# Attention and a quantised feed-forward on one core: unrolled loops, a clock warm-up, the causal mask moved from TensorE to VectorE, and a feed-forward on integer weights

## The chip, the cores and the metric

One core of a Trainium2 chip runs the kernel. The metric is device time in microseconds (us) from launch to end; lower is better. Three plain runs of the kernel before are shown, and one profiled execution, whose trace is read here.

## The reference, cut to what matters

```
x: (8, 512, 128)   w_qkv: (128, 384)   w_gate, w_up: (384, 128) int32   w_down: (128, 384) int32
q, k, v = split(x @ w_qkv, 3)                     # 16 heads of 8
att = softmax(where(causal, q k^T / sqrt(8), -inf))
x = layernorm(x + att v)
gate = x @ (w_gate / 127)^T ; up = x @ (w_up / 127)^T
x = layernorm(x + (silu(gate) * up) @ (w_down / 127)^T)
```

All in float32; both layer norms have eps 1e-5 and no weights.

## The kernel before, in words

Every engine has its instruction stream written out by hand, and semaphores join the streams. Nothing is scheduled by a planner. The work has two phases.

**Attention.** The 8 batches have 16 heads each; four heads make a group, so there are 32 groups (`G`, four to a batch, `n` is the group in its batch). For each group TensorE computes scores twice. First it makes them with the queries on the partitions, only to take each row's maximum: `maxima` fills ten PSUM banks in turn (`k` = 0 to 9, in three real banks `mx_ps`), VectorE's `reduce_group` takes the maxima of each, GpSimd's `split_negmax` splits the negated maximum into two parts, TensorE turns them (`turn_negmax`), ScalarE copies them out, and a DMA (`load_negmax`) puts them as extra rows beside the queries. Two groups later (`LAG`) TensorE makes the scores again with the keys on the partitions and the maximum already subtracted (`scores`, five slots `s` of two banks), ScalarE takes the exponential of a slot (line 563, into `pt`), GpSimd zeroes what lies over the diagonal (`clear_diagonal`, line 843), and TensorE multiplies by the values (`values`, line 376). A column of ones in `vx` gives the row sums. Every second group VectorE divides by them (`normalise`), once a batch GpSimd adds the input (`add_attention`, line 850).

The ten banks of a group hold 16 blocks of 128, 256, 384 or 512 keys (`max_blocks`): banks 0 to 3 one block of 512, banks 4 to 7 one of 384 and one of 128, banks 8 and 9 two of 256. VectorE reduces a bank with one instruction, by chunks of 128 or 256 keys. So that keys behind the query don't count, `maxima` ends each bank with two small matmuls of the constant `tri` (line 366), which add -3e38 over the diagonal of each block.

TensorE's order in a group, `group(...)`, is by slot: `scores` of slot s, `maxima` of banks 2s and 2s+1 of the group two ahead, then in slot 1 `turn_negmax` and the first quarter of `values`, in slot 2 `turn_out` (every second group) and the second quarter, in slot 3 the projections of a later batch (`X`: `project_qk`, or `project_v` with `turn_x`), in slot 4 the rest of `values`. Bank 4 of the maxima uses the PSUM bank of bank 3, since `turn_negmax` and `turn_out` use the other two in between; the others wait for the bank three before.

Two groups' maxima are taken before the first scores (`group(-2)`, `group(-1)`). q and k go through HBM to be laid out as extra terms (`write_parts`, `read_rows` on SyncE's queue); their low parts are made on VectorE (`low_parts`, line 645).

**Feed-forward.** Batches `c` = 0 to 7. VectorE takes the statistics of layer norm 1 (`stats1`) and normalises (`norm1`, line 737), GpSimd takes the inverse deviation (`inverse_deviation`, lines 875 and 877). TensorE turns x1, ScalarE copies it to `x1T`, TensorE makes gate and up in plain float32 (lines 509 and 511, three chunks of 128 hidden units each), ScalarE applies silu, VectorE multiplies (line 747, `hid`), TensorE makes `down` (line 520), VectorE adds x1 and takes statistics (lines 755, 717, 721), and GpSimd normalises (`norm2`, line 885) for the store. GpSimd scales the int32 weights by 1/127 at the start (line 815).

Attention's and the feed-forward's middle batches are hardware loops (`bodies` and `whole_batches` with `Fori`), in which waits and addresses go by registers; the last batches are written out.

## Time and profile before

| | |
|---|---|
| median of 3 runs | 442.48 us (441.56 to 464.72) |
| the profiled execution's own time | 435.57 us |
| its span, first to last instruction | 433.9 us |
| TensorE busy, share of the span | 91% |
| VectorE, ScalarE, GpSimd busy | 64%, 50%, 39% |
| mean granted TensorE clock | 0.895 |

The span and the own time differ by 1.7 us, which lies around the instructions. The profiled execution is 7 us under the median. Matmuls are pipelined, so a busy TensorE isn't one at its peak. [...]

### The profile page before, as it was taken

Reading aid. Unit: us, or ns where it says so; the run is one execution under the profiler, and the core shown is the slowest. Engines: PE = TensorE matmul, PEld = TensorE weight load, DVE = VectorE, ACT = ScalarE, POOL = GpSimd, SP = SyncE. Lnnn points to the kernel's source line nnn. Section 1 sums busy time; section 2 is a strip of 40 time slices with the busy share of each in tenths; the row PEclk is TensorE's granted clock in tenths of the full one; section 3 lists DMA queues with packets and bytes.
Section 4 is the critical chain, followed back from the end, with each engine's and each line's share of the span. In section 5 each row is a group of like instructions: output and inputs, shape, how many; then the busy total and the mean of one; then the engine's idle time right before and its main releaser. Section 6 shows DMA issues by size and latency. Waiting matters only on the chain.

```text
span 433.9 us, 9906 instructions
## 1 busy us (share of the span) xinstructions
PE 393.8 (91%) x3245; PEld 231.4 (53%) x3245; DVE 277.9 (64%) x596; ACT 216.3 (50%) x277; POOL 169.1 (39%) x305
## 2 busy tenths in 40 slices
PE   5289989999999999999999999999999879999990
PEld 3157454455655555555555555555555435576560
DVE  4167434655586777767776876777777336777741
ACT  2114433545475667666566666656666653322220
POOL 8921211222323243333224334223422543776664
PEclk9655655865799999999999999999999999999997
DMA  5820560052505432540543354055100000001001
GB/s 171 264 73 5 215 200 26 4 201 93 148 4 198 132 114 105 188 147 2 196 148 97 130 163 147 2 199 168 53 4 5 26 2 2 25 25 48 26 24 48
DMA packets 33880, 41.48 MB, mean 96 GB/s; under 512 B 3136, under 2 KB 17472, under 8 KB 33856
## 3 DMA queue, kind: packets, MB, share of 16 engines
q1 hardware_dynamic: 33856, 41.17, 29.5%
q8 instruction: 14, 0.23, 0.2%
q14 instruction: 10, 0.08, 0.1%
HBM read 21.76 MB, written 18.87 MB: 94 GB/s over the span
## 4 chain that ended last, share of the span: by engine, by line
PE 70%; DVE 14%; issue 5%; DMA 4%; ACT 2%; SPq 2%; POOL 1%; DVEq 0%; POOLq 0%
PE psum L376 16%; PE psum L357 14%; DVE nm L666 11%; PE psum L346 10%; PE psum L520 5%; PE psum L509 5%; PE psum L511 5%; PE psum L322 5%; PE psum L366 4%; PE psum L312 2%; PE psum L334 2%; DMA scr_k<-parts 2%; PE psum L328 2%; DVE attn L677 1%; DMA xa<-L_attn_x 1%
## 5 line engine op out<-in xcount | busy, mean ns | idle before, releaser
L666 DVE TENSOR_REDUCE nm<-psum 128x1 f32<-128x512 f32 (+2 forms) x320 | 201.1, 684 | 98.6 <-PE psum L366 98.6
L563 ACT ACTIVATE pt<-psum 128x1024 f32<-128x1024 f32 x160 | 159.7, 1024 | 97.7 <-PE psum L346 97.0
L843 POOL TENSOR_SCALAR_AFFINE_SELECT pt<-pt 128x512 f32<-128x512 f32 x128 | 78.9, 634 | 160.0 <-ACT pt L563 159.3
L357 PE MATMUL psum<-kx,qx 33*128 33x128 f32 (+3 forms) x512 | 111.6, 379 | 18.7 <-DMA kx<-scr_k 7.7
L376 PE MATMUL psum<-pt,vx 128*32 128x512 f32 (+3 forms) x1024 | 96.3, 475 | 1.2 <-ACT pt L563 1.0
L346 PE MATMUL psum<-qx,kx 35*128 35x384 f32 (+3 forms) x512 | 88.3, 392 | 0.8 <-DVE parts L645 0.5
L357 PEld LDWEIGHTS psum<-kx,qx 33*128 33x128 f32 x512 | 67.3, 208 | 31.3 <-DVE nm L666 15.9
L346 PEld LDWEIGHTS psum<-qx,kx 35*128 35x128 f32 x512 | 47.3, 202 | 67.1 <-issue 41.8
L366 PE MATMUL psum<-tri 64*128 64x128 bf16 (+1 forms) x640 | 67.6, 227 | 0.0
L366 PEld LDWEIGHTS psum<-tri 64*128 64x128 bf16 x640 | 32.9, 105 | 24.0 <-issue 20.1
L376 PEld LDWEIGHTS psum<-pt,vx 128*32 128x32 f32 x1024 | 24.6, 112 | 21.5 <-issue 7.4
L631 ACT ACTIVATE sg<-psum 128x512 f32<-128x512 f32 x24 | 14.3, 597 | 38.2 <-PE psum L509 38.2
L850 POOL TENSOR_TENSOR res<-res,attn 128x512 f32 (+1 forms) x8 | 10.2, 1272 | 41.5 <-DVE attn L677 21.8
L885 POOL TENSOR_SCALAR yo<-r,mv,rstd 128x128 f32<-128x128 f32 x32 | 25.1, 796 | 2.1 <-POOL rstd L877 2.1
L509 PE MATMUL psum<-x1T,wT 128*128 128x512 f32 x48 | 24.7, 596 | 0.7 <-ACT x1T L623 0.7
L511 PE MATMUL psum<-x1T,wT 128*128 128x512 f32 x48 | 24.5, 592 | 0.0
L520 PE MATMUL psum<-wT,hid 128*128 128x128 f32 x192 | 22.7, 275 | 0.0
L520 PEld LDWEIGHTS psum<-wT,hid 128*128 128x128 f32 x192 | 22.1, 192 | 0.5 <-issue 0.5
L747 DVE TENSOR_TENSOR hid<-psum,sg 128x512 f32<-128x512 f32 x24 | 16.5, 686 | 9.0 <-PE psum L511 8.6
L322 PE MATMUL psum<-xT,wqkv 128*128 128x512 f32 x32 | 20.8, 786 | 0.8 <-ACT xT L542 0.8
L645 DVE TENSOR_TENSOR parts<-psum,parts 128x512 fp32r<-128x512 f32 x16 | 11.1, 691 | 11.8 <-ACT parts L549 11.4
L877 POOL TENSOR_TENSOR rstd<-veps,minus_half 128x4 f32<-128x4 f32 x16 | 16.5, 1034 | 1.3
(58 smaller groups left out, 246.3 us busy)
## 6 DMA issues: line engine op xcount, KB each, us to landing
scr_q<-parts SPq DMA_DIRECT2D x16, 512.0 KB, 3.2
scr_k<-parts SPq DMA_DIRECT2D x16, 512.0 KB, 4.6
qx<-scr_q SPq DMA_DIRECT2D x64, 128.0 KB, 2.8
kx<-scr_k SPq DMA_DIRECT2D x64, 128.0 KB, 2.8
xa<-L_attn_x SPq DMA_DIRECT2D x8, 256.0 KB, 3.0
res<-L_attn_x SPq DMA_DIRECT2D x8, 256.0 KB, 3.5
out<-yo SPq DMA_DIRECT2D x8, 256.0 KB, 2.3
qx<-nm_T SPq DMA_DIRECT2D x64, 8.0 KB
```

The lines of the kernel that those rows point to most:

```text
L322: pe.matmul(pair[:, n, :], wqkv[:, C * n:C * n + C], xT[:], start=True, stop=True).then_inc((q_made, k_made)[n], 1)
L346: last = pe.matmul(pair[:, bank % 2, col:col + width], kx[u][at:at + KS, 2 * g + hh // 2, P * j:P * j + P].bitcast(F32R), qx[u][at:at + KS ...
L357: pe.matmul(bank[:, col:col + width], qx[u][at:at + KM, 2 * g + hh // 2, P * i:P * i + P].bitcast(F32R), kx[u][at:at + KM, 2 * g + hh // 2 ...
L366: last = pe.matmul(dst, tri[at:at + 64, part, :], mask, start=False, stop=(part == 1), skip_group_check=True)
L376: last = pe.matmul(pv_ps[VW * hh:VW * hh + VW, P * j:T], vx[u][:, at:at + VW], pt[g % 2][:, bank, col:col + T - P * j], start=(j == 0 and ...
L509: pe.matmul(psum[:, 1 + k % 2, :], wT[:, 0, P * m:P * m + P], x1T[u][:], start=True, stop=True).then_inc(gate_full, 1)
L511: pe.matmul(psum[:, 3 + k % 2, :], wT[:, 1, P * m:P * m + P], x1T[u][:], start=True, stop=True).then_inc(up_full, 1)
L520: last = pe.matmul(psum[:, 5, C * n:C * n + C], hid[:, m, P * n:P * n + P], wT[:, 2, P * m:P * m + P], start=(m == 0 and n == 0), stop=(m ...
L563: act.activation(pt[g % 2][:, 2 * s:2 * s + 2, :], next_pair(), ACT.Exp, scale=SM_SCALE).then_inc(exp_done, 1)
L666: dve.tensor_reduce(dst, src, AX.X, ALU.max, negate=True).then_inc(mx_reduced, 1)
L843: pool.affine_select(out=blocks, in_=blocks, pattern=[[0, HG], [1, P]], compare_op=ALU.is_ge, fill=0.0, base=0, channel_multiplier=-1).the ...
L885: pool.tensor_scalar(yo[u][:, n, :], r2[:, n, :], mv[:, 1, n, 0:1], rstd[:, 1, n:n + 1], ALU.subtract, ALU.mult).then_inc(yo_made, 1)
```

## The change

**No loops.** `bodies` and `whole_batches` are plain Python loops: every wait is against a constant. Otherwise the attention streams keep their order.

**Inputs sooner.** The loads of x for batches 2 and 3 are issued behind batch 0's `read_rows`, and that of batch b + 4 in group 1 of batch b. Before, batch b + 2 was loaded in group 0 of batch b.

**Zero products first.** `keep_busy(n)` issues n matmuls of zeros (bf16, 128 x 128 by 128 x 512) into the bank of the values: 8 ahead of the first maxima, 3 in each slot of groups -2 and -1, 1 in each slot of group 0. The turning of the feed-forward weights moves ahead of the first maxima; their conversion and the clearing of `vx` move from GpSimd to VectorE.

**The mask.** `tri` and its matmuls are gone. VectorE takes each of the 16 blocks by an instruction of its own that reads PSUM and a mask, adds them, writes the sum times -1 to `masked` (bf16, four buffers) and takes the minimum into `nm`.

**Feed-forward.** The weights stay whole numbers (no 1/127; silu gets it as a scale, and `residual2` as 1/127 squared). x1 is split in two parts, `x1_hi` (ScalarE) and `x1_lo` (VectorE), and gate and up are each two matmuls of type float32r in place of one of float32. `down` of batch c - 1 goes behind the first chunk of batch c, with `hid` in two buffers and x1 in three. `norm1` moves from VectorE to GpSimd; both norms add a negated mean (`minus_mean`, one more small instruction) where they subtracted the mean.

```diff
-                diag = [(col + P * i) // P for _, i, col in blocks]
-                diagonal = bank.rearrange("p (m c) -> p m c", c=P)[:, diag[0]:NB:max(1, diag[-1] - diag[0]), :]
-                for part in range(2):
-                    dst = diagonal[:, :, 64 * part:64 * part + 64]
-                    mask = tri[at:at + 64, 2 + part, 0:64 * len(diag)].rearrange("p (m c) -> p m c", c=64)
-                    last = pe.matmul(dst, tri[at:at + 64, part, :], mask, start=False, stop=(part == 1),
-                                     skip_group_check=True)
                 last.then_inc(mx_full, 1)
...
+            def keep_busy(n):
+                for _ in range(n):
+                    pe.matmul(pv_ps, zeros[:, 0:P], zeros[:], start=True, stop=True, skip_group_check=True)
...
-                dve.tensor_reduce(best[:, :, 5], best[:, :, 0:3], AX.X, ALU.min).then_inc(nm_made, 1)
+                    blocks = max_blocks(k)
+                    for n, (hh, i, col) in enumerate(blocks):
+                        width = P * (i + 1)
+                        count = HG * NB * M + blocks_to(k) + n
+                        if count > 3:
+                            dve.wait_ge(mx_reduced, count - 3)
+                        dve.tensor_tensor_reduce(masked[count % 4][:, 0:width], bank[:, col:col + width],
+                                                 mask[:, T - width:T], -1.0, 3.0e38, ALU.add, ALU.min,
+                                                 best[:, hh, 3 + i:4 + i]).then_inc(mx_reduced, 1)
...
+            def ffn(c, u, first, last_one):
+                gate_up(c, u, 0, first)
+                if not first:
+                    down(c - 1, 1 - u, c == 1)
+                gate_up(c, u, 1, first)
+                if not last_one:
+                    turn_x1(c + 1, 1 - u)
+                gate_up(c, u, 2, first)
...
+            def norm1(c):
+                inverse_deviation(c, 0, mv1_made, ve1_made, mean1_made, rstd1_made)
...
+                for n in range(NB):
+                    pool.tensor_scalar(x1[c % 3][:, n, :], res[:, NB * c + n, :],
+                                       minus_mean[:, 0, n:n + 1], rstd[:, 0, n:n + 1], ALU.add, ALU.mult).then_inc(x1_made, 1)
```

**Where it moves instructions.** On VectorE, one group's maxima. Before (with the low parts of batch 0 ahead of them):

```order
L645 TENSOR_TENSOR parts<-psum,parts 128x512 x2
L666 TENSOR_REDUCE nm<-psum 128x1 x4
L666 TENSOR_REDUCE nm<-psum 128x4 x4
L666 TENSOR_REDUCE nm<-psum 128x2 x2
L668 TENSOR_REDUCE nm<-nm 128x4
```

After, from bank 3 to bank 4 of a group:

```order
L689 ISA masked,nm<-psum,mask 128x512
L689 ISA nm 128x1
L689 ISA masked,nm<-psum,mask 128x384
L689 ISA nm 128x1
L689 ISA masked,nm<-psum,mask 128x128
L689 ISA nm 128x1
```

Eleven instructions of a group become 32: each of the 16 blocks has one that goes over the block, and one that reads the result out to `nm`.

On TensorE, slot 2 of a group with `turn_out`. Before:

```order
L357 MATMUL psum<-kx,qx 128x384
L357 MATMUL psum<-kx,qx 128x128
L366 MATMUL psum<-tri 128x2x64 x2
L357 MATMUL psum<-kx,qx 128x384
L357 MATMUL psum<-kx,qx 128x128
L366 MATMUL psum<-tri 128x2x64 x2
L415 REGISTER_ALU
L312 MATMUL psum<-identf,oT 128x128 x4
L372 REGISTER_ALU
L376 MATMUL psum<-pt,vx 32x384 x4
```

After:

```order
L365 MATMUL psum<-kx,qx 128x384
L365 MATMUL psum<-kx,qx 128x128
L365 MATMUL psum<-kx,qx 128x384
L365 MATMUL psum<-kx,qx 128x128
L320 MATMUL psum<-identf,oT 128x128 x4
L377 MATMUL psum<-pt,vx 32x384 x4
```

The mask matmuls and the register instructions are gone, and nothing else has moved; a whole group loses 20 mask matmuls.

On GpSimd, one batch of the feed-forward. Before:

```order
L875 TENSOR_SCALAR veps<-mv 128x4
L877 TENSOR_TENSOR rstd<-veps,minus_half 128x4
L875 TENSOR_SCALAR veps<-mv 128x4
L877 TENSOR_TENSOR rstd<-veps,minus_half 128x4
L885 TENSOR_SCALAR yo<-r,mv,rstd 128x128 x4
```

After:

```order
L876 TENSOR_SCALAR veps<-mv 128x4
L877 TENSOR_SCALAR minus_mean<-mv 128x4
L879 TENSOR_TENSOR rstd<-veps,minus_half 128x4
L890 TENSOR_SCALAR x_1<-res,minus_mean,rstd 128x128 x4
L876 TENSOR_SCALAR veps<-mv 128x4
L877 TENSOR_SCALAR minus_mean<-mv 128x4
L879 TENSOR_TENSOR rstd<-veps,minus_half 128x4
L901 TENSOR_SCALAR yo<-r,minus_mean,rstd 128x128 x4
```

GpSimd now makes both norms of a batch, and the means' negatives.

## Rows read from the trace of the kernel before

**Rows 1.** The page: busy shares, and TensorE's granted clock in 40 slices.
```profile
PE 393.8 (91%) x3245; PEld 231.4 (53%) x3245; DVE 277.9 (64%) x596; ACT 216.3 (50%) x277; POOL 169.1 (39%) x305
...
PEclk9655655865799999999999999999999999999997
```

**Rows 2.** Windows: PE, PEld, DVE, ACT, POOL busy (instructions), clock, DMA.
```profile
70.00:80.00 10.00, 10.00 (x51) 4.68 (x44) 3.27 (x5) 3.18 (x4) 1.22 (x2) 0.52 0.01 2
...
120.00:130.00 10.00, 9.88 (x94) 5.56 (x97) 7.91 (x15) 6.99 (x11) 2.92 (x6) 1.00 0.01 4
```

**Rows 3.** Windows again: attention at full clock, and the feed-forward.
```profile
120.00:340.00 220.00, 210.43 (x2140) 121.92 (x2143) 164.67 (x294) 139.67 (x174) 74.96 (x146) 1.00 0.34 110
357.00:423.00 66.00, 65.31 (x311) 41.65 (x311) 44.79 (x172) 20.39 (x33) 40.24 (x57) 1.00 0.09 25
```

**Rows 4.** The chain of waits: `project_qk` (start us, us), once a batch.
```profile
75.72 3.73 PE psum L322 x4
...
123.74 1.93 PE psum L322 x4
...
161.43 1.93 PE psum L322 x4
```

**Rows 5.** The timeline, first and last maxima, and attention's last instructions.
```profile
20.48 2.48 DVE L666 TENSOR_REDUCE nm<-psum 128x1 f32<-128x512 f32 x4 [9.58 <-PE psum L366]
...
340.68 0.16 DVE L668 TENSOR_REDUCE nm<-nm 128x4 f32<-128x12 f32 x1
...
355.26 0.60 ACT L575 ACTIVATE oT<-psum 128x512 f32<-128x512 f32 x1 [2.48 <-PE psum L376]
```

**Rows 6.** The timeline, slots 1 and 2 of one group at full clock.
```profile
231.38 2.48 DVE L666 TENSOR_REDUCE nm<-psum 128x1 f32<-128x512 f32 x4 [0.28 <-PE psum L366]
...
233.98 0.50 PE L346 MATMUL psum<-qx,kx 35*128 35x384 f32 x4
...
234.33 0.51 PE L357 MATMUL psum<-kx,qx 33*128 33x384 f32 x4
...
234.62 0.35 PE L366 MATMUL psum<-tri 64*128 64x128 bf16 x4
...
234.89 0.85 PE L376 MATMUL psum<-pt,vx 128*32 128x384 f32 x8
234.94 1.29 DVE L666 TENSOR_REDUCE nm<-psum 128x4 f32<-128x512 f32 x2 [1.07 <-PE psum L366]
```

**Rows 7.** Groups of instructions, shapes apart (busy, mean ns, idle before).
```profile
L677 DVE TENSOR_TENSOR attn<-psum,rsum 128x256 f32<-128x256 f32 x17 | 7.2, 425 | 1.1
...
L673 DVE RECIPROCAL rsum<-psum 128x32 f32<-128x32 f32 x17 | 5.9, 346 | 8.8 <-PE psum L312 8.8
...
L805 POOL TENSOR_SCALAR tri<-tri_f 128x128 bf16<-128x128 f32 x4 | 1.1, 300 | 0.1
```

**Rows 8.** The timeline, one batch of the feed-forward.
```profile
366.16 1.02 PE L509 MATMUL psum<-x1T,wT 128*128 128x512 f32 x2
...
371.31 0.60 PE L312 MATMUL psum<-identf,x 128*128 128x128 f32 x4
...
371.75 2.84 PE L520 MATMUL psum<-wT,hid 128*128 128x128 f32 x24
...
374.43 1.02 PE L509 MATMUL psum<-x1T,wT 128*128 128x512 f32 x2
```

**Rows 9.** The timeline, the end.
```profile
423.96 0.69 DVE L755 TENSOR_TENSOR r<-psum,x 128x512 f32<-128x512 f32 x1 [1.92 <-PE psum L520]
...
425.71 0.38 DVE L721 BATCH_NORM_AGGREGATE mv<-stats 128x2 f32<-128x6 f32 x4 [0.15 <-DVE stats L717]
426.29 0.19 POOL L875 TENSOR_SCALAR veps<-mv 128x4 f32<-128x4 f32 x1 [3.16 <-DVE mv L721]
426.56 1.03 POOL L877 TENSOR_TENSOR rstd<-veps,minus_half 128x4 f32<-128x4 f32 x1
427.83 3.12 POOL L885 TENSOR_SCALAR yo<-r,mv,rstd 128x128 f32<-128x128 f32 x4 [0.24 <-POOL rstd L877]
```

More of the change, by code:

```diff
@@ L71, in max_blocks, with blocks_to @@
     return [(k - 2 * HG, 1, 0), (k - 2 * HG + 2, 1, 256)]
+def blocks_to(k):
+    return sum(len(max_blocks(n)) for n in range(k)) if k >= 0 else blocks_to(MX + k) - HG * NB
 MX_PLACE = (0, 1, 2, 3, 6, 7, 8, 9, 10, 11)
@@ L93, in attention_ffn @@
         identf = sb("identf", [P, P], F32)
-        tri_f = sb("tri_f", [P, 4, P], F32)
-        tri = sb("tri", [P, 4, P], BF16)
+        mask = sb("mask", [P, T], F32)
+        masked = [sb(f"masked{n}", [P, T], BF16) for n in range(4)]
         wqkv = sb("wqkv", [P, 3 * C], F32)
@@ L129, in attention_ffn @@
         x_in = [sem(f"x_in{u}") for u in range(2)]
-        res_in = sem("res_in")
+        res_in = [sem(f"res_in{u}") for u in range(2)]
         w_in = sem("w_in")
@@ L402, in group @@
                         for k in (2 * s, 2 * s + 1):
[L403 removed]
+                            if m > 0 or k > 2:
                                 if k == 5 and NM is not None:
@@ L538, in copy_xt @@
                 act.wait_ge(xt_made, b + 1)
-                if not (isinstance(b, int) and b == 0):
+                if b > 0:
                     act.wait_ge(k_made, b)
@@ L546, in first_parts @@
                     act.wait_ge((q_made, k_made)[n], b + 1)
-                    if n == 0 and not (isinstance(b, int) and b == 0):
+                    if n == 0 and b > 0:
                         act.wait_ge(scr_written, SCR * b)
@@ L552, in copy_v @@
                 act.wait_ge(v_made, b + 1)
-                if not (isinstance(b, int) and b < 2):
+                if b > 1:
                     act.wait_ge(pv_done, NG * b - NG)
@@ L560, in exp_slot @@
                 act.wait_ge(st_full, SLOTS * G + s + 1)
-                if s == 0 and not (isinstance(G, int) and G < 2):
+                if s == 0 and G > 1:
                     act.wait_ge(pv_done, G - 1)
@@ L567, in copy_negmax @@
                 act.wait_ge(nm_turned, m + 1)
-                if not (isinstance(m, int) and m < 2):
+                if m > 1:
                     act.wait_ge(nm_loaded, NM_LOADED * (m - 1))
@@ L654, in reduce_group @@
                         after_k7()
-                    if k == 0 and not (isinstance(M, int) and M < 2):
+                    if k == 0 and M > 1:
                         dve.wait_ge(nm_split, M - 1)
@@ L711, in body @@
                         turn[0] += 1
-            bodies(dve, body)
+            for b in range(B):
+                body(b // 2, b % 2, b + 2 < B, b + 1 < B)
             def norm_stats(src, k, st_made, mv_made, count):
@@ L803, in _ @@
-            pool.wait_ge(tri_step, n)
-            for part in range(4):
-                pool.tensor_scalar(tri[:, part, :], tri_f[:, part, :], 1.0, 0.0, ALU.mult, ALU.add).then_inc(tri_made, 1)
+            pool.affine_select(out=mask[:, T - P:T], in_=mask[:, T - P:T], pattern=[[-1, P]], compare_op=ALU.is_ge,
+                               fill=MASKED, base=0, channel_multiplier=1).then_inc(tri_made, 1)
             pool.memset(minus_half[:], -0.5).then_inc(small_set, 1)
             pool.memset(nm_parts[:], 0.0).then_inc(small_set, 1)
-            for u in range(2):
-                pool.memset(vx[u][:], 0.0).then_inc(v_zeroed, 1)
-                pool.wait_ge(v_zeroed, u + 1)
-                pool.memset(vx[u][:, 0:NB * H * VW].rearrange("p (s w) -> p s w", w=VW)[:, :, VW // 2 + D:VW // 2 + D + 1],
-                            1.0).then_inc(v_ones, 1)
@@ L813, in _ @@
-            pool.wait_ge(wff_in, 48)
-            for n in range(3):
-                pool.tensor_scalar(wdeq[:, n, :], wraw[:, n, :], W_SCALE, 0.0, ALU.mult, ALU.add).then_inc(wff_deq, 1)
-            pool.wait_ge(wff_deq, 3)
             pool.memset(qx[1][:], 0.0).then_inc(rows_set, 1)
@@ L896, in _ @@
+            def ffn(c, u, first, last_one):
+                if not (first or last_one):
+                    norm1(c + 1)
+                if not first:
+                    norm2(c - 1, 1 - u)
+            norm1(0)
+            norm1(1)
             add_attention(B - 1)
-            whole_batches(pool, ffn)
+            whole_batches(ffn)
+            norm2(B - 1, (B - 1) % 2)
 _INS = ["L0_attn_x", "L0_attn_w_qkv", "L0_ffn_w_gate", "L0_ffn_w_up", "L0_ffn_w_down"]
```

299 lines of the change are left out of this document (144 added, 155 removed).

## The prediction

> **What bounds the kernel now.** I read the page first. TensorE is busy 91% of the span, and its granted clock is half or a mixture for the first third; from about 120 us it is full [rows 1]. So two questions come before any other: what sets the pace at full clock, and what the half clock costs.
>
> At full clock [rows 3] TensorE is busy 210.43 of 220 us, VectorE 164.67. The chain of waits shows `project_qk` once a batch; two such starts in the full-clock stretch lie 161.43 - 123.74 = 37.69 us apart [rows 4], so a group takes 9.42 us. Of these TensorE is busy 9.42 x 0.957 = 9.0 and VectorE 9.42 x 0.7485 = 7.05. TensorE is the bound, but VectorE isn't far: it has 2.4 us a group left.
>
> Maxima run from 20.48 to 340.84 us [rows 5], that is 320.4 us for 32 groups; 32 at 9.42 would be 301.4. **The half clock costs 19 us.** A half-clock batch lasts 123.74 - 75.72 = 48.0 us [rows 4], though some of it already ran at full.
>
> The feed-forward repeats every 374.43 - 366.16 = 8.27 us [rows 8], with TensorE busy 65.31 of 66 us [rows 3]. From the last attention copy (355.26 + 0.60 = 355.86, [rows 5]) to the end of the span are 78.0 us.
>
> **TensorE's saving in a group.** Four mask matmuls hold the stream from 234.62 to 234.89, 0.27 us [rows 6]. A group has 12 as wide, 0.81 us, and 8 half as wide, about 0.27 us: 1.1 us. TensorE's need falls from 9.0 to 7.9 us. [...]
>
> **VectorE's cost in a group.** The order shows 16 instructions over the blocks and 16 small reads, for 11 before. The elements are the same, 4 x (512 + 384 + 256 + 128) = 5120. An addition of 512 elements from PSUM takes 0.69 us [rows 9], one of 256 takes 0.425 [rows 7]: 1.035 ns an element, 5.30 us. The fixed part depends on overlap. Two reductions take 1.29 us and four 2.48 [rows 6]: behind another one each adds 0.595, though alone one takes 1.29 - 0.595 = 0.695. So a block costs 0.595 - 0.530 = 0.065 us beyond its elements when it runs behind another, and 0.165 alone. The read isn't in the trace. The nearest rows are small instructions: 0.16 us alone [rows 5], and (0.38 - 0.16) / 3 = 0.073 us in a row of four [rows 9]. I take 0.073, since reads stand in a dense queue; the other end is 0.16, plus 0.10 more if the next block can't overlap the read either. Sum: 5.30 + 16 x (0.065 + 0.073) = 7.5 us. The low parts (2 x 0.69 a batch) and `normalise` (2 x (0.346 + 0.425), [rows 7]) add 2.92 / 4 = 0.73. VectorE needs 8.2 us, more than TensorE's 7.9: **the bound changes engine.** Behind a block that waits for VectorE stand `turn_negmax`, `values` and the next `scores` on TensorE, and behind those ScalarE.
>
> [...]
>
> **Waits that stay.** Bank 4 uses the PSUM bank of bank 3, so TensorE can't fill it until VectorE is done: from its matmul's start to VectorE's are 234.94 - 234.33 = 0.61 us [rows 6], 0.5 without the mask. Now this hides in a wait of 1.07 us; afterwards it is what is left of it. The same refill comes in every second group behind `normalise` (0.25 a group), and the value projection holds TensorE for longer than two full banks last VectorE, about 0.15 a group. A group then takes 8.2 + 0.5 + 0.25 + 0.15 = 9.1 to 9.2 us; I take 9.15, against 9.42. Most of what TensorE saves is thus spent on VectorE. Bounds from this step alone: 8.6 if the waits nearly vanish, 9.42 if they stay as they are.
>
> **The start.** First maxima wait for the round trip of q and k through HBM, which is unchanged: 20.5 us. The feed-forward weights' conversion and the clearing of `vx` go to VectorE, whose wait of 9.58 us before the first maxima [rows 5] covers them. The x loads go ahead in the queue behind `read_rows`; the first negated maximum isn't ready until later. [...] The slices fall from 0.9 to 0.5 from about 10 to 30 us [rows 1], where TensorE, like VectorE, stood still for the round trip, and after `project_qk` of 75.72 us [rows 4] they come back for a while; so I take a TensorE that is kept fed there to hold the full clock throughout, which is worth the 19 us.
>
> **Attention's sum.** 20.5, two groups of maxima alone at 7.5 + 0.5 = 8.0, thirty at 9.15 = 274.5: 311.0 us for the end of the maxima, where it was 340.84. The last two groups have no maxima on VectorE and don't change: 355.86 - 340.84 = 15.0. Attention ends at 326.0.
>
> **Feed-forward.** A float32 product of 512 columns takes (371.31 - 366.16) / 6 = 0.86 us [rows 8]. Two of float32r take its place. The nearest row is 1024 such columns of maxima in 234.62 - 234.33 = 0.29 us [rows 6], two at a time on few rows, so 512 take 0.15 to 0.29; I take 0.22. Twelve are 2.6 us (3.5 at the upper end), turning 0.44, `down` 371.75 to 374.43 = 2.68: TensorE needs 5.7 to 6.6 for 8.27. TensorE is no longer the bound. What is late next is the loop through layer norm 1: statistics until GpSimd starts, 426.29 - 424.65 = 1.6 us (424.65 is the residual's end); inverse deviation 427.83 - 426.29 = 1.54 and the new negated mean 0.2 [rows 9]; four norms; turn 0.6, copy 0.6, low part 0.69, product 0.69, and 0.6 of hand-overs. The norms are the unknown: with subtraction and per-partition operands one takes 3.12 / 4 = 0.78 us [rows 9], while a multiply and add with immediates on the same 128 elements takes 1.1 / 4 = 0.275 [rows 7]. The new form is an add and a multiply, so I take the second, 1.1 us for four. Sum 7.6; overlap at the ends makes me take 7.4. Eight batches save 8 x 0.87 = 7 us. The end saves 2.0 on four norms and pays 0.2 for the mean; the first norm, now on GpSimd behind its last mask, adds 0.5. From 355.86 on: 78.0 - 7 - 1.8 + 0.5 = 69.7 us. Span 326.0 + 69.7 = 395.7; with the 1.7 outside it 397.4. **Forecast: 398 us**, against 435.6 for the profiled execution and 442.5 for the median. The measurement can tell about 2% from no change.
>
> **Rivals.** (1) **GpSimd's norms stay slow**, since per-partition operands and not subtraction make them slow. For it: only the form with immediates is seen fast. Then GpSimd has 2 x (3.12 + 1.74) = 9.7 us a batch and is the bound at 9.8; 8 x 2.4 + 2 + 2 = 23 us more: 421 us.
>
> (2) **The read can't overlap its block** (the slower side). Place: between each of 512 pairs on VectorE, now the bound. Price: 0.16 in place of 0.073 is 0.09 us, 46 us in all, 444 us; if the next block waits as well, 0.19 us, 97 us, 495 us. In the middle, at 0.13, it is 465. It turns the change slower from 44.5 / 512 = 0.087 us a block on. For it: the result exists only after the last element. Against it: all neighbours in this trace overlap.
>
> (3) **The clock falls in mid-attention.** TensorE's busy share drops from 96% to some 86%, and the mask matmuls, which kept it fed, are gone. From 75.72 to 123.74 about 20 us were at full clock, so 28 us at half did the work of 17.7, 1.58 times as long. TensorE's 7.9 would be 12.5 us, 3.3 over a group; over half of the groups that is 50 us: 448 us. Against it: windows at half clock had TensorE busy too (10.00 of 10, [rows 2]), so its share isn't what decides, and it held from 120 us on.
>
> (4) **The mask as second operand halves the rate.** [...] It would be 5.3 x 32 = 170 us more, 567 us. [...]
>
> (5) **The waits vanish**: groups of 8.6 us and batches of 6.6: 375 us.
>
> **Chances.** Forecast 0.46 (its own range 384 to 415), rival 1 0.12, rival 2 0.20, rival 3 0.12, rival 4 0.04, rival 5 0.06. Faster by over 2% (under 433.6): the forecast, 5, nearly all of 1, half of 3 and a little of 2: 0.71. Within 2%: 0.10. Slower, over 451.3: 0.19, mostly 2 and 4. The range goes from 378, between rival 5 and the forecast, to 450, past rivals 1 and 3 and the low end of 2.
>
> **What would show it.** Clock 1.00 in nearly all slices; first maxima at 20 to 21 us; block and read together about 0.138 us over the elements; VectorE near 90% in attention with TensorE waiting for it; a batch of attention 36.6 us; four norms on GpSimd in 1.1 us; a feed-forward batch of 7.4. I am wrong if the read takes 0.16 us or holds its neighbours, or if the clock isn't full behind the first groups.

## The result, and the profile after

The changed kernel takes 491.5 us (median of four; 482.0 to 501.3), the kernel before beside it 442.0 (436.2 to 464.7). Ratios are taken between the faster executions of both kernels, here 482.0 and 485.3 against 436.2 to 442.5: 1.099, 95% interval 1.077 to 1.121. The forecast was 398 us. The kernel before scatters by itself: of its 41 executions in this study 19 took 431 to 445 us and 22 took 454 to 497, and the longer ones had the lower mean clock (444 us with 0.87, 497 us with 0.73).

The profiled execution took 482.0 us, with a span of 480.3. Its page, to be laid beside [rows 1]:

```profile
PE 435.2 (91%) x2646; PEld 237.9 (50%) x2648; DVE 298.0 (62%) x1252; ACT 217.2 (45%) x277; POOL 163.9 (34%) x325
...
PEclk9897569558999955965556555985675559899998
```

TensorE has 600 matmuls fewer in its records and was busy 41 us longer. The last row says why. Before, the clock was mixed until 120 us and then full (1.00) to the end. Now it goes up and down until 400 us. The mean is 0.74 for 0.895. Even the start, where the change has its zero products, isn't at full clock throughout (columns as in [rows 2], the clock is the third from the right):

```profile
20.00:30.00 10.00, 9.66 (x35) 3.42 (x34) 7.40 (x33) 0.00 (x0) 0.16 (x1) 0.69 0.63 171
30.00:40.00 10.00, 9.03 (x47) 4.37 (x47) 8.78 (x41) 3.32 (x5) 1.34 (x5) 0.99 0.02 4
40.00:50.00 10.00, 9.70 (x36) 4.54 (x39) 7.22 (x31) 5.43 (x7) 2.45 (x6) 0.67 0.46 171
```

In windows of 2 us it is 0.50 from 20 to 26 us, full from 28 to 38, and 0.50 again from 40 to 46. Ahead of the first maxima (19.71 us) TensorE had stood 2.83 us for the DMA of k: the eight zero products didn't reach that far.

The timeline has `project_qk` once a batch of attention, as [rows 4]:

```profile
117.82 1.98 PE L330 MATMUL psum<-xT,wqkv 128*128 128x512 f32 x4
...
154.36 1.98 PE L330 MATMUL psum<-xT,wqkv 128*128 128x512 f32 x4
...
200.58 1.98 PE L330 MATMUL psum<-xT,wqkv 128*128 128x512 f32 x4
```

The first two are 36.54 us apart, and between them the clock was full. Before, it was 37.69. The next are 46.2 us apart; later (the chain of waits, 253.49 to 305.00) it is 51.5, mostly at half clock. Windows of that one good batch and of two stretches behind it (columns as in [rows 2]):

```profile
117.82:154.36 36.54, 33.41 (x288) 17.49 (x284) 30.15 (x136) 24.05 (x31) 12.79 (x25) 1.00 0.41 132
...
166.00:194.00 28.00, 27.81 (x148) 15.12 (x148) 15.13 (x72) 11.82 (x15) 7.66 (x15) 0.51 0.37 116
...
210.00:255.00 45.00, 44.90 (x233) 23.75 (x233) 24.84 (x116) 19.04 (x23) 10.69 (x21) 0.50 0.31 98
```

Read across: at full clock TensorE is busy 91% of the time (before 96%, [rows 3]) and VectorE 83%. At half clock TensorE is busy 99 to 100% and the others wait for it: from 210 to 255 us ScalarE waits 21.8 us for the scores and VectorE 17.9 us for the maxima. So the 99 to 100% stand here with a clock of 0.50 to 0.51, and are no sign that nothing is wrong.

What TensorE did before the clock fell at about 166.1 us, in windows of 1 us:

```profile
164.00:165.00 1.00, 0.45 (x6) 0.25 (x4) 0.59 (x2) 0.76 (x1) 0.00 (x0) 1.00 1.02 377
165.00:166.00 1.00, 0.77 (x10) 0.57 (x8) 0.71 (x5) 0.68 (x2) 0.57 (x1) 1.00 1.02 379
166.00:167.00 1.00, 0.88 (x6) 0.66 (x10) 1.00 (x7) 0.61 (x1) 0.88 (x3) 0.54 1.03 383
```

This is a group without projections, in slots 3 and 4. TensorE first stood 0.55 us for `normalise` and then 0.35 us for a maximum:

```profile
164.75 0.50 PE L365 MATMUL psum<-kx,qx 33*128 33x384 f32 x4 [0.55 <-DVE attn L700]
...
166.12 0.79 PE L365 MATMUL psum<-kx,qx 33*128 33x256 f32 x2 [0.35 <-DVE nm L689]
```

In windows of 1 us the clock falls from full nine times in attention. The first three falls (39.8, 50.0, 63.7 us) are in groups with projections; the other six (84.2, 166.1, 207.0, 261.7, 319.7, 353.8 us) are all in groups without.

VectorE, the answer to [rows 5 and 6]. Each block has its pass and its small read:

```profile
20.63 0.69 DVE L689 CUSTOM_DVE_ANT_0 masked<-psum,mask 128x512 bf16<-128x512 f32 x1 [4.34 <-PE psum L365]
21.25 0.08 DVE L689 DVE_READ_ACCUMULATOR2_ANT nm<- 128x1 f32 x1
21.25 0.69 DVE L689 CUSTOM_DVE_ANT_0 masked<-psum,mask 128x512 bf16<-128x512 f32 x1
...
132.28 0.68 DVE L689 CUSTOM_DVE_ANT_0 masked<-psum,mask 128x512 bf16<-128x512 f32 x1
132.89 0.08 DVE L689 DVE_READ_ACCUMULATOR2_ANT nm<- 128x1 f32 x1
132.89 0.69 DVE L689 CUSTOM_DVE_ANT_0 masked<-psum,mask 128x512 bf16<-128x512 f32 x1
```

The pass of a full block takes 0.69 us, and the next one starts 0.61 us behind it, at the very moment at which the read starts. The passes over 512, 384, 256 and 128 elements take 687, 555, 419 and 285 ns on the mean, 134 ns for 128 elements, which is 0.54 us for 512 (the prediction's estimate was 0.53); the read takes 83 ns. With the 0.53, pass and read together cost 0.61 - 0.53 = 0.08 us over the elements.

The feed-forward, the answer to [rows 8], and its norms, the answer to [rows 9]:

```profile
429.50 0.66 PE L320 MATMUL psum<-identf,x 128*128 128x128 f32 x4 [1.29 <-POOL x L890]
...
429.91 0.48 PE L521 MATMUL psum<-x_hi,wT 128*128 128x512 f32 x1
...
437.08 0.66 PE L320 MATMUL psum<-identf,x 128*128 128x128 f32 x4 [0.94 <-POOL x L890]
...
437.49 0.48 PE L521 MATMUL psum<-x_hi,wT 128*128 128x512 f32 x1
...
475.90 1.74 POOL L901 TENSOR_SCALAR yo<-r,minus_mean,rstd 128x128 f32<-128x128 f32 x4 [0.24 <-POOL rstd L879]
```

A batch takes 437.08 - 429.50 = 7.58 us for 8.27, and TensorE now waits about 1 us in it for GpSimd's norms. Four norms take 1.74 us. Attention ends at 405.93 + 0.60 = 406.5 us (before 355.9), the whole at 480.3. The loss is all in attention.

### The profile page after: what moved, and what is told of

Same layout as the page of the kernel before. It is cut to its first block, busy times and chain, and to the rows that moved or that the text cites. A ratio compares the mean times of both kernels' runs of the same rounds, so it can differ in the third digit from the quotient of the medians.

```text
span 480.3 us, 8390 instructions
## 1 busy us (share of the span) xinstructions
PE 435.2 (91%) x2646; PEld 237.9 (50%) x2648; DVE 298.0 (62%) x1252; ACT 217.2 (45%) x277; POOL 163.9 (34%) x325
## 4 chain that ended last, share of the span: by engine, by line
PE 41%; DVE 7%; POOL 5%; issue 4%; ACT 1%; POOLq 0%; DVEq 0%
PE psum L377 14%; PE psum L354 9%; PE psum L365 9%; PE psum L320 3%; POOL x L890 3%; DVE masked L689 2%; POOL rstd L879 2%; PE psum L330 2%; DVE stats L754 2%; PE psum L342 1%; PE psum L336 1%; PE psum L533 1%; DVE pt L789 1%; ACT x_hi L647 1%; DVE mv L758 1%
## 5 line engine op out<-in xcount | busy, mean ns | idle before, releaser
L689 DVE CUSTOM_DVE_ANT_0 masked<-psum,mask 128x384 bf16<-128x384 f32 (+3 forms) x512 | 218.6, 487 | 124.9 <-PE psum L365 105.6
L365 PE MATMUL psum<-kx,qx 33*128 33x384 f32 (+3 forms) x512 | 122.2, 430 | 12.5 <-DVE nm L689 5.7
L377 PE MATMUL psum<-pt,vx 128*32 128x512 f32 (+3 forms) x1024 | 126.2, 603 | 1.0 <-ACT pt L586 1.0
L689 DVE DVE_READ_ACCUMULATOR2_ANT nm<- 128x1 f32 x512 | 42.3, 83 | 0.0
L533 PE MATMUL psum<-wT,pt 128*128 128x128 f32 x192 | 22.9, 276 | 1.5 <-DVE pt L789 1.5
L533 PEld LDWEIGHTS psum<-wT,pt 128*128 128x128 f32 x192 | 22.5, 192 | 2.8 <-DVE pt L789 2.3
L524 PE MATMUL psum<-x_lo,wT 128*128 128x512 f32 x48 | 20.4, 426 | 2.0 <-DVE x_lo L770 2.0
L521 PE MATMUL psum<-x_hi,wT 128*128 128x512 f32 x48 | 21.3, 445 | 0.7 <-ACT x_hi L647 0.7
L789 DVE TENSOR_TENSOR pt<-psum,sg 128x512 f32<-128x512 f32 x24 | 16.0, 672 | 2.9 <-ACT sg L655 2.0
L320 PE MATMUL psum<-identf,oT 128*128 128x128 f32 x68 | 15.7, 373 | 0.8 <-ACT oT L598 0.8
```

What stands on the lines that cost most here:

```text
L320: last = pe.transpose(dst[:, P * n:P * n + P], src[:, P * n:P * n + P], identf[:])
L365: last = pe.matmul(bank[:, col:col + width], qx[u][at:at + KM, 2 * g + hh // 2, P * i:P * i + P].bitcast(F32R), kx[u][at:at + KM, 2 * g + ...
L377: last = pe.matmul(pv_ps[VW * hh:VW * hh + VW, P * j:T], vx[u][:, at:at + VW], pt[g % 2][:, bank, col:col + T - P * j], start=(j == 0 and ...
L521: pe.matmul(psum[:, bank + k % 2, :], w, x1_hi[u][:].bitcast(F32R), start=True, stop=False)
L524: pe.matmul(psum[:, bank + k % 2, :], w, x1_lo[u][:].bitcast(F32R), start=False, stop=True).then_inc(full, 1)
L533: last = pe.matmul(psum[:, 5, C * n:C * n + C], hid[u][:, m, P * n:P * n + P], wT[:, 2, P * m:P * m + P], start=(m == 0 and n == 0), stop= ...
```

## The experiments

Before each expectation stands the edit. "A wide zero product" is a matmul of zeros, 128 x 128 by 128 x 512 in bf16, into the bank that `scores` is about to fill; it computes nothing that is used.

**1. Is it the clock, and which part of the change loses it?** Four kernels ran side by side.

The changed kernel with a wide zero product ahead of the scores of every slot:

```diff
             def scores(u, g, s):
                 pair = next_pair()
+                pe.matmul(pair[:, 0, :], zeros[:, 0:P], zeros[:], start=True, stop=True, skip_group_check=True)
```

> The changed kernel with one zero product more (bf16, 128 x 128 by 128 x 512) ahead of the scores in every slot of attention, in the bank that the scores then overwrite. Theory A (the clock fell since the mask matmuls no longer fill TensorE in between): the product puts as much work back, the granted clock is above 0.95 and the time is near 390 us, from groups of 7.9 to 8.5 us. Theory B (the clock falls where TensorE waits for VectorE, and filling elsewhere doesn't help): the clock stays near 0.74 and the time is 490 us or more, since the product takes 0.4 us a slot at half clock. Theory C (the unrolled streams or the new order of transfers): as B.

The changed kernel with zero matmuls in the shape and place of the mask matmuls (64 rows, in the banks of the maxima):

```diff
+                for part in range(2):
+                    none = zeros[at:at + 64, 0:64 * len(diag)].rearrange("p (m c) -> p m c", c=64)
+                    last = pe.matmul(dst, zeros[at:at + 64, 0:P], none, start=False, stop=(part == 1), ...)
```

> The changed kernel with the two mask matmuls of each bank put back in their place and shape, but with zeros in them, so that TensorE's stream is that of the kernel before while VectorE keeps the new masking. Theory A: the clock is back above 0.9 behind the start and the time is 390 to 400 us (groups of 9.0). Theory B: VectorE still makes TensorE wait, the clock stays below 0.8, and the time is 480 to 500 us. Theory C: as B.

The kernel before, its mask matmuls left out and nothing in their place, so that keys behind the query count in the maxima:

```diff
-                    last = pe.matmul(dst, tri[at:at + 64, part, :], mask, start=False, stop=(part == 1), ...)
```

> The kernel before with its mask matmuls left out, so that keys behind the query count in the maxima; all else, VectorE's reductions and the loops too, is as before. Theory A: the clock that was full from 120 us on now falls in attention, the mean is 0.70 to 0.80, and the time is 450 to 480 us although TensorE has 1.1 us a group less to do. Theory B: VectorE is as fast as it was, the clock stays full in the steady part, and the time is about 405 to 430 us. Theory C: as B, 405 to 430.

The changed kernel with VectorE's reductions of before. The maxima take no mask at all:

```diff
-                        dve.tensor_tensor_reduce(masked[count % 4][:, 0:width], ...)
+                    dve.tensor_reduce(dst, src, AX.X, ALU.max, negate=True)
```

> The changed kernel with VectorE's ten reductions a group as before and no mask at all, so that keys behind the query count in the maxima. Theory A: no change of the clock, 0.70 to 0.78, and 470 to 495 us. Theory B: TensorE waits less for VectorE, the clock is above 0.9, and the time is near 380 us. Theory C: as A.

| | median us (runs) | mean clock of each run |
|---|---|---|
| wide zero products | 427.3 (423.5 to 433.8) | 0.95 to 0.99 |
| mask-shaped zeros | 463.3 (436.4 to 478.1) | 0.80 to 0.91 |
| before, no mask matmuls | 472.3 (460.2 to 478.5) | 0.74 to 0.78 |
| after, old reductions | 471.7 (467.8 to 492.9) | 0.69 to 0.77 |
| the kernel before, same chip | 444.7 (443.0 to 497.1) | 0.73 to 0.87 |

The first kernel does more work than the changed one and is 64 us faster by the medians (all its executions are under 434 us, all of the changed kernel's over 482). Against the kernel before it is 0.956 (0.950 to 0.963). Its page and a window of its attention:

```profile
PEclk9858999999999999999999999999999998999997
```

```profile
80.00:340.00 260.00, 254.43 (x1989) 122.41 (x1988) 194.97 (x872) 161.97 (x194) 85.36 (x167) 1.00 0.32 103
```

So the clock is the loss: held at 1.00, even a kernel with more work is faster than before. The third kernel changes nothing but the mask matmuls, and in the stretch in which the clock was 1.00 before [rows 3] it is 0.73:

```profile
120.00:340.00 220.00, 211.69 (x1415) 112.10 (x1416) 139.11 (x248) 120.39 (x148) 63.59 (x124) 0.73 0.33 108
```

TensorE had less to do and a batch took 44.4 us (the chain of waits, 162.72 to 207.17) for 37.69. That all of its four executions are at a clock of 0.74 to 0.78, while about half of those of the kernel before are at 0.87 and more, makes me blame the mask matmuls' absence; one execution would not have, since the kernel before also had executions at 0.73 to 0.75. The fourth says that VectorE's new instructions aren't what loses the clock: with the old reductions it is at 0.69 to 0.77. Its median is 20 us under the changed kernel's, but the executions overlap, so a smaller share of VectorE isn't excluded. The second says that putting matmuls of that shape back isn't enough to be safe: 436 us once, 478 at worst.

**2. How much has to be put in?** In `scores`, for the changed kernel: the wide product only `if s in (0, 2, 3)`; five of 256 columns; mask-shaped zeros with 128 rows for 64. And the kernel before with 16 zero products at the start, three a slot in groups -2 and -1 and one a slot in group 0.

> The changed kernel with the wide zero product ahead of the scores in slots 0, 2 and 3 alone, three a group where the first such run had five, which held the clock at 1.00 in attention with groups of 9.95 us. Theory A (the clock needs a certain amount of work on TensorE, wherever it comes from): three are 1536 columns at 128 rows; if that is enough, the clock is above 0.95, groups take 9.1 us, and the time is 400 to 405 us; if it isn't, the clock is at 0.75 to 0.9 and the time 430 to 480. Theory A2 (what counts is that no slot runs thin): the bare slots 1 and 4 have the values, so the clock holds too, same numbers. Theory B (waits for VectorE decide, and five products only bridged them): the clock falls, 450 us or more.

> The changed kernel with a zero product of 256 columns ahead of the scores in all five slots: 1280 columns at 128 rows a group, half of the first such run. Theory A: a dose question; if half is enough, the clock is above 0.95 and groups of 8.9 us give near 395 us; if not, 0.8 and 440 to 470 us. Theory B: the clock falls, 450 us or more.

> As the run with zeros in the mask matmuls' place and shape, but the products have 128 rows in place of 64; columns, number and place are the same, so TensorE's time is too. That run sat between the states (436 to 478 us). Theory A by rows (what counts is how much of the array a product fills): the clock now holds above 0.95 and the time is 395 to 410 us. Theory A by time alone (what counts is how long TensorE streams): no difference, 435 to 478 us.

> The kernel before with the zero products of the start alone: 16 ahead of the first maxima, 3 in each slot of groups -2 and -1, 1 in each of group 0. All else is the kernel before. My forecast's term says that these 19 us come back: clock near 1.00 from 25 us on, 415 to 425 us. The rival reading, after the changed kernel fell back to half clock at 46 us though it had the same products: they lift the clock only while they last, it falls again by 50 us, and the time is 435 to 450 us, as before.

They took 485.0, 454.7, 654.4 and 476.8 us (medians), at mean clocks in the profiled executions of 0.83, 0.82, 0.64 and 0.84. None holds the clock. The 128-row form is slow even at full clock. In the timeline one bank of maxima, two matmuls in series, takes 0.32 and 0.44 us, and its zeros 0.22. In the changed kernel, with nothing between them, two banks of this shape take 0.34 us together (120.07 to 120.41 us):

```profile
309.07 0.40 PE L365 MATMUL psum<-kx,qx 33*128 33x256 f32 x2
309.39 0.29 PE L374 MATMUL psum<-zeros 128*128 128x128 bf16 x2
309.61 0.50 PE L365 MATMUL psum<-kx,qx 33*128 33x256 f32 x2
310.05 0.29 PE L374 MATMUL psum<-zeros 128*128 128x128 bf16 x2
```

From 309.07 to 310.26 us two banks with their zeros take 1.19 us. The same in the kernel with zeros of 64 rows takes 0.56 (153.41 to 153.97 us). The expectation took TensorE's time as the same for 64 and for 128 rows; it isn't. The kernel puts every second bank's operands on partitions 64 and up. In the changed kernel two products of 512 columns, one from each half, start together at 131.14 us and are done in 0.40, and one alone takes 0.49 (131.65 us). With the zeros of 128 rows the second bank's products start only at 309.61 us, 0.54 behind the first bank's: here the two banks no longer run at the same time. How much of the 654 us is this and how much the clock wasn't separated.

The last one speaks on the step that failed in my prediction. The kernel before, started with zero products, has the full clock from 30 to 42 us and loses it there again (0.57 to 0.63 from 42 to 60). Its 476.8 us (462.4 to 479.8) are no gain on the 464.7 (443.7 to 490.8) of the kernel before beside it, and neither expectation had it that slow. It also lost the clock at about 247 us, in a stretch in which TensorE did little (windows):

```profile
230.00:240.00 10.00, 9.39 (x105) 5.15 (x100) 7.50 (x14) 6.00 (x7) 2.92 (x6) 1.00 0.58 214
240.00:250.00 10.00, 4.69 (x51) 3.24 (x48) 4.05 (x8) 3.69 (x5) 2.23 (x5) 0.86 0.37 111
250.00:260.00 10.00, 10.00 (x59) 5.38 (x58) 4.50 (x8) 3.33 (x4) 2.02 (x3) 0.50 0.46 133
```

Here TensorE stood 3.4 and 1.8 us, and from 150 to 160 us, where the clock was already at 0.50, 2.37 and 1.77 us. At none of the four did it wait for a semaphore that the trace shows; the timeline calls it "issue". This kernel and the kernel before have loops. The profiled execution of the kernel before has no such stop; nor have those of the changed kernel and of two unrolled ones with wide zero products, in every slot and in both groups without projections. That the stops come from the loop's instructions, and that they make the scatter of the kernel before, fits this but was not tested.

**3. Which products, which slots, which start?** The wide products in slots 0 to 3; in both groups of a batch that have no projections (`g in (3, 0)`); in every slot but without the change's 8 + 30 + 5 zero products at the start; and in the kernel before.

> Four wide zero products a group in place of five (none in slot 4, where TensorE already has the values of two key blocks). Theory P (the clock needs the stream of TensorE without thin places, and slot 4 isn't one): the clock stays at 1.00 as with five products, and a group costs 0.3 us less where TensorE is the bound (9.95 to about 9.6): 427 - 32 x 0.3 = 418 us. Theory Q (there is no spare: a fifth product less lets the clock fall now and then, as three did): mean clock 0.85 to 0.95 and 440 to 465 us.

> Five wide zero products, but only in the groups in which no projections run (two of each batch's four), in which the clock was seen to fall. Theory P (the fall starts in those groups' thin places alone): clock 1.00 all through, two of four groups 7.9 to 8.5 us, two 9.95, attention some 20 to 25 us shorter than with products in all: about 405 us. Theory Q (groups with projections are no better fed in the mean of a stretch): the clock falls in them, mean 0.75 to 0.88, and the time is 445 to 475 us.

> The version with five wide zero products in every group, without the 8 + 30 + 5 zero products of the change at the start. Theory P (the start's products matter as such): the first groups run at half clock for 20 to 40 us more, 8 to 15 us in all: 435 to 442 us. Theory Q (what holds or raises the clock is the steady stream alone, and the start's products bring at most a few us): 427 to 431 us.

> The kernel before, with the same five wide zero products a group. Theory P (such products hold the clock in either kernel, and the kernel before loses it only where it isn't kept fed): clock 1.00 from the first groups on, a group of 9.42 + 5 x 0.3 = 10.9 us since TensorE is its bound, attention 20.5 + 32 x 10.9 + 15 = 385 us, and with 78 us behind it 465 us, with hardly any scatter between runs. Theory Q (its stops, in which TensorE waits for its own instructions, cost it the clock whatever it computes): stretches at half clock stay, and it is 480 us or more.

| | median us (runs) | clock, profiled |
|---|---|---|
| slots 0 to 3 | 455.8 (450.6 to 468.1) | 0.85 |
| groups without projections | 427.7 (415.8 to 437.0) | 0.89 |
| every slot, no products at the start | 427.5 (426.4 to 433.0) | 0.95 |
| the kernel before, every slot | 472.4 (465.4 to 475.2) | 0.90 |

Four products aren't four fifths of five: theory Q. Without the start's products the time is the same (427.5 for 427.3, though on another chip), and the profiled executions agree: `project_qk` of the same batch starts at 66.29 us without them and at 66.43 with them, although the clock is 0.50 from 20 to 40 us without. So those 43 products, the change's own means, bring nothing that can be seen here. In the kernel before the wide products cost more than they bring (472.4 us, against 457.2 for the kernel before beside it): TensorE, busy 210.43 of 220 us without them [rows 3], is its bound, and stretches at half clock stay.

The second row is the telling one. It has half as many products as the kernel of experiment 1, and its page:

```profile
PEclk9899667999999999999999999955596576999998
```

From 80 to 280 us the clock is full without a break. It falls at about 281.3 us, and it comes back late:

```profile
278.00:280.00 2.00, 2.00 (x24) 1.13 (x23) 1.93 (x13) 1.62 (x3) 1.66 (x4) 1.00 0.73 231
280.00:282.00 2.00, 1.61 (x7) 0.52 (x10) 2.00 (x7) 1.66 (x3) 0.27 (x2) 0.82 0.01 2
282.00:284.00 2.00, 2.00 (x14) 0.82 (x8) 0.23 (x2) 0.00 (x0) 0.00 (x0) 0.50 0.06 16
```

By the timeline this is slot 1 of a group of the last batch but one that has no zero products and whose value projection comes only in slot 3 (288.20 us), behind a wait of 0.27 us for VectorE. The group behind it is the first that has neither zero products nor projections, since no later batch is left to project, and the last batch (from about 318 us) has two more. The first kernel of the next pair puts products into these three, and leaves the place where the fall began as it is.

**4. The place.** Wide products in all groups without projections, the last batch's too, and in the first three groups (`if X is None or G < 3`). The same number of products, but only in the groups with projections (`g in (1, 2)`). And the changed kernel with mask-shaped zeros and the old reductions together.

> Five wide zero products in every group without projections, the last batch's groups 1 and 2 among them, and in the first two groups with projections. Theory P (the clock falls where a group has neither projections nor zero products): full clock from the first groups to the end of attention, groups of 9.95 and 7.9 to 8.5 us by turns, attention's end near 326 us, and 400 to 410 us in all, with under 2% between runs. Theory Q (what held from 80 to 280 us in the run before this one was luck of a marginal stream): stretches at half clock somewhere in 60 to 300 us, and 415 to 440 us.

> Five wide zero products only in the two groups of each batch that have projections, as many as in the run that left the clock full for 200 us, in the other places. Theory P (the groups without projections are where it falls): mean clock 0.70 to 0.78, the time 480 to 500 us, no better than the changed kernel. Theory Q (it is the number of products over a batch that counts, wherever they stand): mean clock 0.88 or more and 415 to 440 us.

> The changed kernel with both things put back that it took from the kernel before in the maxima: VectorE's reductions of whole banks, and on TensorE matmuls of zeros in the place, shape and number of the mask matmuls. It leaves out the mask's numbers in the maxima. No loops, early inputs, the start's zero products and the new feed-forward stay. Theory A (the clock is lost with the mask products): the clock is near 1.00 from 60 us on, a group 9.4 us, 425 to 440 us. Theory R (something else in the changed kernel's stream, the missing register instructions or its evener pace, also costs the clock): mean clock under 0.85 and 455 us or more.

The first took 421.7 us (417.4 to 422.0), 0.953 of the kernel before (0.939 to 0.967). The second took 490.3 (479.8 to 490.8), no better than the changed kernel with no zero products in attention's steady part. Their pages:

```profile
PEclk9899977999999999999999959999999996999998
```

```profile
PEclk9799876588555975795559555985696589899998
```

This pair tells the place, for whole groups: **the clock is mostly lost in the groups without projections**. In the second kernel's trace all seven falls behind 70 us are in such groups, as the last six of the changed kernel were. Projections are float32 products of 128 rows one behind the other (four take 1.98 us at full clock); most other products of a group are of 33 and 35 rows or 32 columns. It wasn't quite as expected: the first kernel still lost the clock at 58 and 242 us, so 421.7 in place of 400 to 410. Both falls are in groups with projections. The one at 242 is at the very place of the fall at 281.3 us above: slot 1 of a group with the value projection and without zero products, behind a wait of 0.27 us. The one at 58 is in a group that has both zero products and projections. So "without projections" is where most falls are, not a condition. The batch at full clock is 37.87 us.

The third took 455.2 us (447.5 to 456.8), on the side of theory R. Its clock was full from 130 to 285 us and half from 80 to 120 and in the last batch:

```profile
PEclk9898969555599999999999999655559858899997
```

Of its four falls before 300 us two (39.0, 59.5) are in groups with projections and two (80.0, 288.2) in groups without. Its 455.2 us lie inside what the kernel before took beside it (440.4 to 487.3, median 463.4), so this run doesn't show whether the unrolled stream with both parts put back holds the clock worse than the kernel before, or as badly. Experiment 1 points at the mask matmuls' absence; this run and its second kernel say that putting their like back doesn't make the clock safe.

**5. Down to the slot?** As the first kernel of 4, with two products more in the groups with projections: in slots 0 and 1 (`if thin or s < 2`), or in slots 3 and 4 (`if thin or s > 2`), where the projections stand.

> As the run with zero products in all groups without projections, and two more in slots 0 and 1 of the groups with projections. Theory P, down to the slot (the clock falls in the stretch that has neither projections nor zero products, which in these groups is slots 0 to 2): full clock from 40 us to the end of attention, 412 to 420 us, with hardly any scatter. Theory Q (only the number over a group counts): the same as the other kernel of this pair.

> The same number of zero products, but the two more stand in slots 3 and 4 of the groups with projections, beside the projections. Theory P, down to the slot: the clock still falls now and then in the first slots of such a group, 420 to 432 us: no better than without them (421.65) and a few us worse for their own time. Theory Q: as the other one, clock 1.00 and 412 to 420 us.

418.4 us (416.5 to 421.6) and 426.2 (423.0 to 429.7). The times are those of theory P, but the trace doesn't bear out its reason. From 80 us to the end of the maxima both have a clock of 1.00 and batches of 38.5 us, although the second leaves bare the place of the falls at 242 and 281.3 us. They differ in the first 80 us. The first fell at 45 us, but was back before 60. The second stood 2.36 us for a DMA at 57 us and ran at half clock from 59 us to past 67, where its `project_qk` took 3.78 us:

```profile
57.10 0.39 PE L351 MATMUL psum<-zeros 128*128 128x512 bf16 x1 [2.36 <-DMA qx<-nm_T]
```

```profile
56.00:58.00 2.00, 0.90 (x5) 0.40 (x5) 0.00 (x0) 0.04 (x1) 0.17 (x1) 1.00 0.49 149
58.00:60.00 2.00, 2.00 (x8) 0.85 (x6) 1.71 (x5) 1.98 (x2) 0.00 (x0) 0.75 0.95 258
60.00:62.00 2.00, 2.00 (x9) 0.20 (x8) 0.82 (x4) 0.27 (x1) 0.63 (x1) 0.50 0.43 129
```

Whether the slot within a group matters stays open. The first of the two is by its median the fastest version of this study: the slowest of its four executions (421.6) is 10 us under the fastest of the seven that the kernel before ran beside it (431.4 to 486.0).

```profile
PEclk9899699999999999999999999999999996999998
```

Where does it gain on the profiled execution of the kernel before (span 433.9)? Its attention ends at 341.51 + 0.60 = 342.1 us, not 355.9, though its batch of 38.50 us is longer than the 37.69 of before: all 13.8 us come from the start, where before ran at half clock, and the mask's move has been eaten up by the products that replace it. The feed-forward and the end take 417.0 - 342.1 = 74.9 us for 78.0.

## Why the prediction was wrong

**The step that failed** stands under "The start": "so I take a TensorE that is kept fed there to hold the full clock throughout". In the sum that put the loss of the clock in attention at nothing, and the start's gain at 19 us. Measured, the clock was 0.69 from 20 to 30 us in spite of the zero products, 0.99 from 30 to 40, and it fell in the first group that had scores to make (39.8 us) and eight times after that. Attention ended 80.5 us later than forecast (406.5 for 326.0 us). The start's products didn't decide it either way: without them, but with products in attention, nothing was lost (427.5 against 427.3 us). The prediction's own sign of being wrong, a clock that isn't full behind the first groups, is the one that came. And rival 3, which had the mechanism with its cause ("the mask matmuls, which kept it fed, are gone"), got a chance of 0.12 by two bad arguments. "its share isn't what decides" took windows at half clock with TensorE fully busy as evidence that feeding it doesn't help; but the busy share there comes with products stretched by the half clock: the four of `project_qk` take 3.73 us at 75.72 us and 1.93 at 123.74 [rows 4]. And "it held from 120 us on" was an observation of the stream with mask matmuls, used for one without them.

**Rival 3's size.** It priced a half-clock group at 3.3 us over a group, and half of the groups. Measured: (51.5 - 36.54) / 4 = 3.7 us, and the attention's excess of 406.5 - 326.0 = 80.5 us is that of 21 to 22 of the 32 groups. The price was near; the share of the groups was too small. The mechanism that it names, the missing mask matmuls, is borne out by experiment 1 as a part: no run separates what the unrolled loops and the new order of transfers do to the clock.

**The group at full clock.** Forecast 9.15 us, a batch of 36.6; measured 36.54. The sum was right by two errors. VectorE costs 0.08 us a block over the elements, not 0.138, so it is busy 30.15 / 4 = 7.5 us a group and not 8.2. TensorE is busy 33.41 / 4 = 8.35 and not 7.9. The 1.1 us that the mask matmuls were to give back came out as 9.0 - 8.35 = 0.65. The bound didn't change engine, then: TensorE is still the busier, and it stands 9.14 - 8.35 = 0.8 us a group. The gain, 1.15 us a batch, is as small as forecast.

**Rival 2 is refuted.** The read of the accumulator takes 0.083 us and starts with the next pass (21.25 us), and a pass starts while the one before has 0.07 us to go (0.69 - 0.62). Neither the read nor the next pass waits for the end of the one before, as the reductions of before didn't (0.695 us long and 0.595 apart, [rows 6]). Rival 4, the mask as second operand at half the rate, is refuted as well: a block of 512 takes 0.69 us with it, and a reduction over 512 without it took 0.68 in the kernel before.

**The feed-forward.** Forecast 7.4 us a batch, measured 7.58. The norm takes 0.447 us on GpSimd, between my 0.275 and the 0.78 of rival 1. From attention's end on it is 480.3 - 406.5 = 73.8 us, forecast 69.7: 1.4 of the 4.1 are eight batches of 0.18, 0.6 the four last norms. The rest was not taken apart; at the passage from attention TensorE stood for layer norm 1 and then ran at half clock for some 3 us:

```profile
408.00:412.00 4.00, 2.24 (x9) 1.48 (x10) 2.52 (x11) 2.43 (x3) 1.95 (x6) 0.98 0.00 0
412.00:416.00 4.00, 4.00 (x14) 2.98 (x13) 2.19 (x4) 1.85 (x4) 2.41 (x4) 0.59 0.00 0
```

**The forecast's sum** therefore held wherever the clock held: 36.54 for 36.6 a batch, first maxima at 20.6 for 20.5. It would have given 398 us plus the feed-forward's 4. What it lacked was the condition under which it was true, and no run in this study kept the changed kernel at that clock without paying 1.3 to 3.3 us a batch for it.

## What to carry to other kernels

When an edit takes work from TensorE, ask what clock the rest will run at: look at where the stream is thinnest, not at its mean, and price the half clock over most of the phase rather than as a remote case (here it was the excess of 21 to 22 groups of 32). A busy share of 99% at a clock of 0.50 was no proof here that TensorE was fed before the clock fell; compare the times of the same instructions at either clock. To test for it, put useless wide products into the stream: five a group brought this kernel from 491.5 to 427.3 us and its clock from 0.74 to 0.97, so the clock was what it had lost by. Then find the few places that need them.

## What the runs showed of the hardware

- The granted clock fell although TensorE was busy 91% in the batch before (117.82 to 154.36 us, at 1.00). The fall came in a group without projections, after waits of 0.55 and 0.35 us. The other five falls behind 70 us were in groups without projections too, the three before 70 us in groups with them.
- Five wide zero products in each of two groups of four kept the clock full for 200 us; the same number in the other two groups left it at 0.76 on the mean. One costs 0.32 us of stream (200.24 to 200.56 in the kernel of experiment 1), but a group with five took only (39.8 - 36.54) / 4 = 0.8 us more, and TensorE's idle time in a batch went from 36.54 - 33.41 = 3.1 us to 0.8 (39.00 of 39.82 us busy): a part of their time fell into waits.
- Zero matmuls of 128 rows between products of 33 rows: two banks of maxima with their zeros take 1.19 us at full clock, against 0.56 with zeros of 64 rows and 0.34 with none. With 20 such pieces a group the kernel took 654 us, against 463; its mean clock was lower too (0.64 for 0.80).
- The zero products at the start didn't bring the full clock at once: in the changed kernel it was 0.50 from 20 to 26 us while they ran, and in the first kernel of experiment 1, with the same start, 0.50 from 20 to 30 and 0.69 from 30 to 40. The eight ahead of the first maxima took 1.89 us at a clock of 1.00 (14.99 to 16.88 us), the last of them 0.38, so (1.89 - 0.38) / 7 = 0.216 us each.
- GpSimd's per-partition add and multiply on 128 x 128 takes 0.447 us, the subtract and multiply before it took 0.78 [rows 9].
